# The way into an attention loop rebuilt (order of statistics, banks, transfers), and the keys of pairs 5 and 11 projected as [feature, token]

## What is computed

```
x = _layernorm(h); Q = x @ Wq; K = x @ Wk; V = x @ Wv      # 6 heads, DQK = 128, DV = 64
Q, K = _xpos(Q, +1), _xpos(K, -1)                          # x1*cos - x2*sin, x1*sin + x2*cos, halves of 64
out = (Q K^T * decay mask) V                               # causal, no softmax
h = h + (groupnorm(out) * silu(x @ Wg)) @ Wo
z = _layernorm(h) P; top 4 of 64 experts in each of 8 groups; h = h + FFN(z)
```

## Time and profile before

| | |
|---|---|
| median of 3 runs | 892.36 us (890.64 to 892.42) |
| profiled execution | 895.4 us, of which the span in the trace is 893.6 us |
| PE busy | 847.4 us (95% of the span) |
| DVE, ACT, POOL busy | 661.7, 593.3, 528.8 us |
| mean granted TensorE clock | 0.982 of full speed |

### The profile page before, as it was taken

How to read it: one execution, slowest core, us unless ns; L and a number is a source line. 1 busy time by engine, 2 the same in 40 slices (tenths; PEclk the granted TensorE clock), 3 DMA queues, 4 the chain that set the end, 5 groups by cost and what they waited for, 6 DMA issues and landing times.

```text
span 893.6 us, 16290 instructions
## 1 busy us (share of the span) xinstructions
PE 847.4 (95%) x5430; PEld 393.1 (44%) x5430; DVE 661.7 (74%) x1609; ACT 593.3 (66%) x901; POOL 528.8 (59%) x481
## 2 busy tenths in 40 slices
PE   8799999999999986998999999999999999999997
PEld 3477777777778755222223222322232223222222
DVE  5666666565476776888878887888788887877774
ACT  2243333335542472989897989798979897988784
POOL 0456565445365633575957595759575767575552
PEclk9999999999999998799999999999999999999998
DMA  9600002000000078889878887988788888889772
GB/s 257 235 1 1 2 2 76 2 1 1 1 2 16 15 113 197 252 251 264 247 225 258 270 252 234 262 269 246 248 249 273 251 270 249 267 268 285 246 253 98
DMA packets 90116, 154.28 MB, mean 173 GB/s; under 512 B 30329, under 2 KB 56377, under 8 KB 89644
## 3 DMA queue, kind: packets, MB, share of 16 engines
q1 hardware_dynamic: 90034, 153.25, 58.3%
HBM read 138.96 MB, written 15.83 MB: 173 GB/s over the span
## 4 chain that ended last, share of the span: by engine, by line
PE 75%; ACT 11%; DVE 7%; DMA 3%; issue 3%; SPq 1%; POOL 0%; DVEq 0%; POOLq 0%; ACTq 0%
PE ps L917 17%; PE ps L854 17%; PE ps L512 5%; PE ps L893 5%; PE ps L535 3%; PE ps L520 3%; PE ps L608 3%; PE ps L545 2%; PE ps L599 2%; ACT ring L1253 2%; DMA wbc<-w_rows 2%; PE ps L577 2%; PE ps L687 1%; PE ps L656 1%; PE ps L708 1%
## 5 line engine op out<-in xcount | busy, mean ns | idle before, releaser
L1958 POOL TENSOR_TENSOR ring<-ring,wbc 128x512 f32<-128x512 f32 x192 | 245.5, 1280 | 151.6 <-ACT ring L1262 139.7
L1740 DVE TENSOR_TENSOR ring<-ps,ring 128x1024 f32<-128x1024 f32 x192 | 234.7, 1222 | 81.0 <-PE ps L893 52.2
L854 PE MATMUL ps<-zst,w1st 99*128 99x512 bf16 x768 | 213.5, 389 | 21.4 <-ACT ring L1253 10.7
L1253 ACT ACTIVATE ring<-ps 128x1024 f32<-128x1024 f32 x192 | 196.7, 1025 | 16.7 <-PE ps L854 16.6
L917 PE MATMUL ps<-ring,w2cur 128*32 128x512 f32 x1536 | 205.2, 607 | 0.0
L1264 ACT ACTIVATE ps<-ps 128x512 f32<-128x512 f32 x192 | 112.9, 588 | 55.0 <-PE ps L854 54.9
L1743 DVE TENSOR_TENSOR ring<-ps,wbc 128x512 f32<-128x512 f32 x192 | 130.9, 682 | 1.7 <-DMA wbc<-w_rows 1.6
L854 PEld LDWEIGHTS ps<-zst,w1st 99*128 99x128 bf16 x768 | 61.5, 98 | 143.3 <-issue 44.5
L1262 ACT ACTIVATE ring<-ps 128x512 f32<-128x512 f32 x192 | 116.4, 606 | 0.1
L1806 POOL TENSOR_TENSOR s2q<-s2q,rope 128x768 f32<-128x768 f32 x24 | 43.1, 1820 | 90.4 <-ACT s2q L1061 90.4
L893 PEld LDWEIGHTS ps<-wst,sel 32*128 32x128 bf16 x384 | 18.1, 91 | 148.9 <-DVE ring L1740 94.0
(11 more groups left out here) (192 smaller groups left out, 1290.1 us busy)
## 6 DMA issues: line engine op xcount, KB each, us to landing
wbc<-w_rows SPq DMA_DIRECT2D x192, 512.0 KB, 5.6
w2cur<-in_w SPq DMA_DIRECT2D x48, 256.0 KB, 4.8
w_parts<-wp SPq DMA_DIRECT2D x72, 64.0 KB, 3.3
zst<-z_parts SPq DMA_DIRECT2D x72, 64.0 KB, 5.0
w1st<-w_parts SPq DMA_DIRECT2D x12, 256.0 KB
wst<-w_parts SPq DMA_DIRECT2D x24, 128.0 KB, 4.2
z_parts<-zp SPq DMA_DIRECT2D x6, 384.0 KB, 5.5
wst<-w_parts SPq DMA_DIRECT2D x24, 96.0 KB, 4.0
```

Of the source, the lines that this page charges most:

```text
L854: return pe.matmul(bank(to), w1st[0:99, 4 * a + j, col:col + P], zst[0:99, (i // 2) % 2, j, :], start=True, stop=True)
L1253: act.activation(ring[:, slot:slot + 2, :].rearrange("p a n -> p (a n)"), ps[:, 0:2 * BLK], ACT.Gelu_apprx_tanh).then_inc(s["duo_gelu"], 1)
L1740: dve.tensor_tensor(v, ps[:, WBANK * 512:WBANK * 512 + 1024], v, ALU.mult).then_inc(s["duo_done"], 1)
L1958: pool.tensor_tensor(ring[:, slot, :], ring[:, slot, :], wbc[:, g % 4, 1, :], ALU.mult).then_inc(s["tri_done"], 1)
```

## The change

It has these parts.

- **Front.** DVE takes statistics of tiles 0 and 1 alone before pair 0 is normalised; the other 22 follow while PE works. Instead of two fillers of 512 columns (`keep_warm(2, 4)`) there is one of 256.
- **Banks of pair 0.** `keys(0)` goes to banks 4 to 7 and waits for no reader of the queries. `values(0)` and `gates(0)` come right behind; they wait for the readers of the queries, and `xn_turn(1)` after them for those of the keys. On DVE the two rotations of the queries stand between the statistics; on ACT the swaps come ahead of the second root.
- **Keys of pairs 5 and 11** are projected like queries (`turned_keys`). ACT swaps halves (`swap_keys`, four copies more), DVE multiplies by cosines alone (two products for six), the sines are multiplied on POOL for pair 5 and on DVE for pair 11 (`sine_keys`), POOL's sum writes `kT` itself. `turn` and `keep` of these pairs are gone. For pair 11 POOL adds the queries first.
- **Tail.** DVE: the variances after `mark(3)`, both masks together. PE: `gn_spread` right behind `gn_mean`, `turn_gates(3)` behind `turn_x2`. POOL writes the parts of tile 3 into `zp2` and so doesn't wait for the store of tile 2; ACT's `z_high(2)`, which uses `zp2`, waits for the stores of four tiles. SP: rows and parts of tile 3 and parts of tile 2 are stored after `attention_over`, the fourth `spread` is issued ahead of `zst`, and the second row of ones, with a semaphore of its own, last; the FFN's first product doesn't wait for it.
- **FFN.** One filler product more (`keep_clock(1, PBANK)`) ahead of a score product in the third tile's groups.

```diff
@@ SP
-                             t["ones"][:, 1024 * m:1024 * m + 1024]).then_inc(s["ld_late"], 16)
+                             t["ones"][:, 1024 * m:1024 * m + 1024]).then_inc(s["ld_ones" if m else "ld_late"], 16)
...
             store_rows(2)
-            store_rows(3)
-            store_gates(2)
-            store_gates(3)
             sp.wait_ge(s["aq"], TILES)
             sp.wait_ge(s["ak"], TILES)
             attention_over(sp)
             sp.wait_ge(s["wo_s"], PAIRS // 2)
             sp.dma_start(sel[:, :, :].rearrange("p q n -> p (q n)").bitcast(F32), t["sel"]).then_inc(s["ld_sel"], 16)
+            store_rows(3)
+            store_gates(2)
+            store_gates(3)
...
-            for g in range(3):
+            for g in range(4):
                 spread(g)
...
-            load_ones(1)
             load_w1(sp, 1)
+            load_ones(1)
@@ PE
-            keep_warm(2, 4)
+            keep_warm(1, 4, 256)
...
+            def turned_keys(k):
+                pe.wait_ge(s["rq"], 2 * k + 2)
+                both_tiles(k, 0, QK)
+                pe.wait_ge(s["sq"], 2 * k + 2)
+                both_tiles(k, 1, QK)
+                both_rests(k, QK).then_inc(s["k_full"], 1)
...
             def values(k):
-                pe.wait_ge(s["rk"], 2 * k + 1)
+                    pe.wait_ge(s["rq"], 2)
+                    pe.wait_ge(s["sq"], 2)
+                else:
+                    pe.wait_ge(s["rk"], 2 * k + (1 if plain(k) else 2))
+                if not plain(k):
+                    pe.wait_ge(s["sk"], 2 * (k // CH) + 2)
...
             def heads(k, x):
-                pe.wait_ge(s["kept"], 2 * k + 2)
+                if plain(k):
+                    pe.wait_ge(s["kept"], turns_before(k) + 2)
+                else:
+                    pe.wait_ge(s["ak"], 2 * k + 2)
+                    pe.wait_ge(s["o_out"], 2 * k)
+                    pe.wait_ge(s["st_out"], sums_before(k))
+                    if k < CH:
+                        pe.wait_ge(s["flip_s"], 2 * k)
...
-            pe.wait_ge(s["ld_late"], 16 * 3)
+            pe.wait_ge(s["ld_late"], 16 * 2)
@@ ACT
+            def swap_keys(k, x):
+                hd = DQK // 2
+                src = ps[:, 1280 * x:1280 * x + QK].rearrange("p (h n) -> p h n", n=P)
+                act.wait_ge(s["k_full"], k + 1)
+                if x == 1:
+                    act.wait_ge(s["rk"], 2 * k + 1)
+                act.wait_ge(s["ak"], 2 * (k - 1) + x + 1)
+                act.copy(t2k[0:hd, x, :, :], src[hd:P, :, :])
+                act.copy(t2k[hd:P, x, :, :], src[0:hd, :, :]).then_inc(s["sk"], 1)
...
+                if blk == 2:
+                    act.wait_ge(s["w_stored"], 48 * 4)
@@ DVE
+            def rotate_turned_keys(k, x):
+                c = k % CH
+                dve.wait_ge(s["k_full"], k + 1)
+                dve.wait_ge(s["ak"], 2 * (k - 1) + x + 1)
+                dve.wait_ge(s["turned"], turns_before(k - 1) + x + 1)
+                dve.wait_ge(s["st_full"], sums_before(k - 1) + x + 1)
+                if x == 0:
+                    dve.wait_ge(s["sk"], 2 * (k // CH) + 1)
+                dve.tensor_tensor(t1k[:, x, :, :], ps[:, 1280 * x:1280 * x + QK].rearrange("p (h n) -> p h n", n=P),
+                                  _mid(rope[:, c, 2, :], H), ALU.mult).then_inc(s["rk"], 1)
@@ POOL
+                if k == 5:
+                    sine_keys(k, 0)
+                    sine_keys(k, 1)
+                if k == 11:
+                    rotated_queries(k, 0)
+                    rotated_queries(k, 1)
                 rotated_keys(k, 0)
                 rotated_keys(k, 1)
```

More of the change, by code:

```diff
@@ L781, in _ @@
                 values(k)
+                if k == 0:
+                    gates(0)
+                    pe.wait_ge(s["rk"], 2)
                 if k + 1 < PAIRS:
@@ L1037, in keep @@
             def keep(k, x):
-                act.wait_ge(s["turned"], 2 * k + x + 1)
+                if not plain(k):
+                    return
+                act.wait_ge(s["turned"], turns_before(k) + x + 1)
                 if k > 0:
@@ L1192, in _ @@
                     z_mid(0)
+                if not plain(k):
+                    swap_keys(k, 0)
+                    swap_keys(k, 1)
                 if k + 1 < PAIRS:
@@ L1688, in _ @@
                     row_stats(5)
-                    dve.wait_ge(s["st2"], 6)
-                    variances(4, 12)
             largest(3, 0, S)
             mark(3, 0, S)
+            dve.wait_ge(s["st2"], 6)
+            variances(4, 12)
+            mask(PAIRS - 1, 0)
+            mask(PAIRS - 1, 1)
+            shifts(4, 4, 12)
             chosen_exps(3)
-            mask(PAIRS - 1, 0)
-            shifts(4, 4, 12)
-            mask(PAIRS - 1, 1)
+            outputs(PAIRS - 1, 0)
             normaliser(3)
-            outputs(PAIRS - 1, 0)
             group_stats(PAIRS - 1, 0)
@@ L1860, in high_part @@
                 pool.wait_ge(s["wT_done"], tile + 1)
-                if tile > 0:
+                if tile > 0 and tile != 3:
                     pool.wait_ge(s["w_stored"], 48 * before(tile))
```

162 lines of the change are left out of this document (106 added, 56 removed).

## The result

The changed kernel takes 886.16 us (median of 14 runs, 883.46 to 889.02); the kernel before, on the same chips, 892.2 (14 runs). The ratio is 0.993, with a 95% interval of 0.9913 to 0.9947: 6 us faster, where I had forecast 18 and a range that ended at 880.5. Its profiled execution took 885.89 us with a span of 883.8, against 895.4 and 893.6 before.

What follows compares the result with a forecast made beforehand. PE was taken to bound the loop (busy 257.5 of 260 us), with idle PE at the two joints. Terms summed to 18.4 us: 895.4 profiled to 877.0, or 874.0 from the 892.36 median; forecast 874.5, range 870.5 to 880.5.

Steps and rivals of the forecast that it cites:

- the price of DVE's variances in the front: Front, DVE between query rotations: variances take 1.5 us, plus 1.2 us for one meeting with POOL.
- the time at which SP would issue the loads for the FFN: Joint before the FFN: spreads go out at 332.5, all four by 335, `zst` by 340, `wst` by 341.
- Front, -6.3: Start to `turn(0)`: PE's pauses for rotations shrink, `turn(0)` at 37.8 against 44.05; 6.3 us saved, bounds 4.5 and 7.8.
- Pair 5, -1.4: Attention pair 5: two turns of 0.7 us each leave PE; 1.4 us saved, bounds 0 and 1.5.
- Rival B: Pairs 5 and 11: a turned-key chain over three engines is late, 2 to 4 us less gain, 878; chance 0.14.
- Pair 11, 0: Attention pair 11: PE's savings against DVE some 1.3 us late, got back at the masks; net 0, bounds +1.5 and -1.5.
- Group norm, -1.7 and -0.8: Tail: second small product right behind the first saves 1.7 us; big normalisation without POOL saves 0.8, bounds 0 and 1.
- DMA wait, -6.4: Before the FFN: PE's 6.7 us wait for a DMA into `zst` goes, less 0.3; 6.4 us saved, bounds 2.5 and 6.7.
- rival A: Before the FFN: the wait for DMAs stays and the clock falls again, 6 us less gain, 880.5; chance 0.13.
- FFN start, -1.1: First FFN groups: full clock makes ACT the bound, first GELU 0.5 us sooner; 1.1 us saved, bounds 0 and 2.
- The filler at i = 2, -0.7: FFN: added filler may spare the 0.62 clock at 416 to 420; 0.7 us saved, bounds +0.9 and -1.5.

Runs made afterwards that it cites:

- weights first: Changed kernel with SP issuing the first half of the first-layer weights ahead of the store of the first z parts: 883.06 us, ratio 0.9888 to the kernel before.

## Why the prediction was wrong

Two steps of the sum failed most: the price of DVE's variances in the front, and the time at which SP would issue the loads for the FFN.

**Front, -6.3.** In the two first traces 3.3 (49.60 to 46.30). The step that failed is the price of the variances: I took 1.5 us and one meeting with POOL at 1.2; they met it twice and took 4.5. Moving them out of the way gave 2.2 us (heads(0) at 44.2 in the mean of six traces with the short filler and early variances, 46.4 in seven with late ones). The clock cost the queries 2.7 us, not 1.5. And the kernel before was sized on one execution: in its three traces heads(0) stood at 49.60, 47.84 and 48.79, so the front's gain is 2.3 us in the mean. By the Trainium skill, "GPSIMD Engine Reference" (1. Specifications), DVE contends with POOL for SBUF where an instruction has two SBUF inputs or runs in a 2-port mode. The trace agrees for `lns<-stats`, with two inputs, at 1.71 us. The one behind it has one tensor input and took 1.70, and so has the product of 1.83 us in the earlier trace rows that I had counted as two-input contention; in which mode these ran, no trace here shows.

**Pair 5, -1.4.** Right in mechanism, 0.95 in size: the values waited 0.30 us for the swapped copy, and the keys cost 0.1 more. Rival B's chain was not late here.

**Pair 11, 0.** 0.8 lost (25.76 against 24.98), inside my bounds. I had the turned keys bring DVE 1.3 us late into the top-4 and the order of the masks give that back; the keys cost 2.2, and the new orders gave 1.4. I had seen POOL's sum come at the heads, and not that the weights of tile 2, on which `mark(3)` waits, and the z part for SP are queued behind it on POOL. This was rival B with the place right and the price wrong: `sine_keys` took 1.89 us for both, not 1.8 each. And it lacked its larger half, the z part that holds the first-layer weights.

**Group norm, -1.7 and -0.8.** From the first small product to the first normalisation 4.45 us became 3.17, so 1.3. The big normalisation took 2.02 in place of 3.10, somewhat better than forecast, but DVE then waited 1.4 us for POOL's distances. From the first small product to the end of PE's last projection 22.28 us became 20.78: 1.5 of the 2.5 were left.

**DMA wait, -6.4.** This step failed: "since tile 3 is split early, they go out at 332.5". That put the first spread 14.1 us ahead of PE (ready at 346.6 in the same count); in the changed kernel it was 10.6 (333.58, and 344.16 for the end of the last projection). The split was early, done at 326.1, but SP's three stores of it took 4.63 us, since the DMA engines were full with the first-layer weights at about 115 GB/s, and their start hung on POOL. With the weights first the same stores took 1.38 us, the first spread left 14.8 us ahead of PE, and the wait for `zst` was gone. The other half of my step was about right: from the first spread to the landing of `zst` it took 13.5 us against the 13 of the sum, with 275 GB/s at 334 to 347. `wst` came 1.7 us later still, so PE waited 2.9 + 1.2 us: 2.6 won in place of 6.4. This is rival A's outcome, by another mechanism. Also, PE was ready later than I had said: its last projection ended at 344.16, 5.0 us earlier than before, where I had forecast 10.2.

**FFN start, -1.1.** Nothing: in every trace the clock was at half within 6 us of the FFN's first product, with a pause before it or without. **The filler at i = 2, -0.7:** right and larger. Each of the three traces without it has a stretch at half clock between 398 and 421, costing 1.7 us of full-speed time (two in the second trace of before); none of the fifteen with it has one there. Four of these have one at 364 to 397, all with spread gates that came late. Others lie at 309 to 331 (five traces) and at 758 to 778 (three).

**The sum.** Up to the FFN's first product the two first traces differ by 8.8 us: front 3.3, pair 5 1.0, pair 11 -0.8, group norm and the rest of the tail 1.5, wait for `zst` 3.8. Forecast were 16.6. Behind it they differ by 1.0, with the 1.2 for `wst` lost in it, where 1.8 were forecast. That is the 9.8 of the spans. The medians differ by 6. I had taken 3 us off for the profiled execution of before lying over its median, while two of my terms were sized on what was long in just that execution (keys at half clock, 1.7 us more than in the second trace, and a DMA wait of 6.7 in place of 5.1). That may be the same 3 us counted twice; it is argued, not shown, since the second trace was as long in the end. Of the 3.8 us between spans and medians, 3.2 are the profiled execution of before over its median (895.4 against 892.2); what made it long stays open.

## What to carry to other kernels

Where a queue of transfers follows a gate in program order, look for the engine that really opens the gate: here an exchange of two lines on SP was worth about 0.4% in the changed kernel, as much as half the change, with intervals that just overlap, because the first large load stood behind a store whose data came from POOL. In the kernel before it was worth nothing, since there another wait ended last. When PE gets faster, ask which of the other engines' chains (POOL's, the DMA engines') now ends last, and price them from that moment on; bytes that are full-time work for the DMA engines can be put into idle slices, but not after them. Sizes of single terms should come from two traces, above all where the clock is at half in one: a stretch of 3.4 us more or less costs 1.7 us.

## What the runs showed of the hardware

The low clock in the front begins at 15 to 18 us in all traces and lasts until 21.0, 22.4, 22.5, 23.0 and 26.6 us with long fillers, 24.5 to 27.6 with the short one (thirteen traces). Five traces have a second such stretch between 29.8 and 39.4, and others with the same pauses have none. So the fillers help often and not always, and I don't know what decides. In "TensorE: Matmul & The Clock Gate" (Part 1, What's actually happening) the Trainium skill says that the moment of release varies from run to run for one kernel; the two traces of the kernel before agree, with 21.0 and 22.5. The time from the issue of the last load of `zst` to its landing, where PE waited for it, ranged from 6 to 11.7 us for the same DMAs in nearly the same place.
